# A graph attention layer with a dense 4096 x 4096 mask: half of each mask unit's transposes move from TensorE to the DMA queue in the last two chunks

## What is computed

```
h = relu(layernorm(x))
Wh = h @ W                                   # 4096 x 128
e  = leaky((Wh @ a1)[:, None] + (Wh @ a2)[None, :])   # leaky slope 0.2
e  = where(adj > 0, e, -9e15)                # adj: 4096 x 4096 int32, 64 MB
out = x + elu(softmax(e, axis=1) @ Wh)
```

## Time and profile before

| | |
|---|---|
| median of 3 runs | 248.27 us (248.07 to 249.45) |
| the profiled execution | 247.97 us |
| its span, first to last instruction | 246.2 us |
| PE, DVE, ACT, POOL busy | 92%, 80%, 69%, 24% |
| transfers of `adj` | 64 of 1 MB |

### The profile page before, as it was taken

The page is one execution under the profiler, slowest core; times in us unless marked ns, Lnnn a source line. Parts: engine busy times, 40 slices in busy tenths (PEclk is TensorE's granted clock), DMA queues, the critical chain, the costliest instruction groups (busy, mean ns, idle before and its releaser), DMA issues.

```text
span 246.2 us, 8267 instructions
## 1 busy us (share of the span) xinstructions
PE 227.2 (92%) x3736; PEld 221.2 (90%) x3736; DVE 196.3 (80%) x259; ACT 169.8 (69%) x149; POOL 59.0 (24%) x48
## 2 busy tenths in 40 slices
PE   6958999599999999999999999999999999999770
PEld 2748899599999999999999999999999999999770
DVE  4997988437776898889888988898889888988935
ACT  3699975696799999994996679219976795020051
POOL 3647027798000070300000560000003700040000
PEclk9997999999999999999999999999999999999996
DMA  6999999999999999999999999999999200020002
GB/s 216 352 387 387 385 388 386 386 319 337 304 333 325 335 388 386 386 385 385 397 387 386 388 386 388 386 386 376 385 387 384 89 3 0 3 88 3 0 3 91
DMA packets 36521, 71.92 MB, mean 292 GB/s; under 512 B 1282, under 2 KB 1924, under 8 KB 36484
## 3 DMA queue, kind: packets, MB, share of 16 engines
q1 hardware_dynamic: 35520, 69.74, 78.6%
q10 hardware_dynamic: 964, 1.64, 1.8%
HBM read 69.27 MB, written 2.10 MB: 290 GB/s over the span
## 4 chain that ended last, share of the span: by engine, by line
PE 77%; DVE 10%; issue 4%; POOL 4%; ACT 2%; DMA 1%; DVEq 0%; POOLq 0%
PE acc L834 21%; PE acc L835 21%; PE acc L836 21%; PE mask_t L817 11%; DVE words L610 3%; POOL v L330 2%; POOL val L333 2%; DVE stats L547 1%; DMA x_sb<-in_x_dram 1%; PE acc L805 1%; ACT v L508 1%; PE acc L796 1%; DVE wh_sb L573 1%; PE mask_t L785 1%; DVE hp L718 1%
## 5 line engine op out<-in xcount | busy, mean ns | idle before, releaser
L610 DVE SCALAR_TENSOR_TENSOR words<-g_row,gq_word,mask_t 128x1024 f32<-128x1024 f32 x128 | 161.1, 1277 | 36.7 <-PE acc L836 18.8
L834 PE MATMUL acc<-val,words 128*128 128x129 f16 x992 | 170.6, 220 | 1.2 <-DVE num L618 0.9
L835 PE MATMUL acc<-val,words 128*128 128x129 f16 x992 | 170.6, 220 | 0.0
L836 PE MATMUL acc<-val,words 128*128 128x129 f16 x992 | 170.6, 220 | 0.0
L420 ACT ACTIVATE mask<-raw,step_bias 128x2048 uint8<-128x2048 int32 x63 | 121.7, 1993 | 21.9 <-DVE x_sb L626 13.5
L834 PEld LDWEIGHTS acc<-val,words 128*128 128x128 f16 x992 | 97.1, 98 | 1.5 <-DVE words L610 1.0
L835 PEld LDWEIGHTS acc<-val,words 128*128 128x128 f16 x992 | 97.1, 98 | 0.1
L836 PEld LDWEIGHTS acc<-val,words 128*128 128x128 f16 x992 | 97.1, 98 | 0.0
L817 PE MATMUL mask_t<-ident_b,mask 128*128 128x128 bf16 x512 | 34.7, 222 | 1.4 <-ACT mask L420 1.4
L817 PEld LDWEIGHTS mask_t<-ident_b,mask 128*128 128x128 bf16 x512 | 30.8, 100 | 1.6 <-ACT mask L420 1.5
L358 POOL TENSOR_TENSOR hp<-num,rz 128x1024 f32<-128x1024 f32 x3 | 5.7, 1898 | 106.3 <-DVE rz L621 106.3
(11 more groups left out here) (94 smaller groups left out, 147.1 us busy)
## 6 DMA issues: line engine op xcount, KB each, us to landing
raw<-in_adj_dram SPq DMA_DIRECT2D x64, 1024.0 KB, 13.8
x_sb<-in_x_dram SPq DMA_DIRECT2D x8, 256.0 KB, 5.7
out_dram<-x_sb ACTq DMA_DIRECT2D x3, 512.0 KB, 7.5
out_dram<-x_sb SPq DMA_DIRECT2D x2, 128.0 KB, 1.9
out_dram<-x_sb SPq DMA_DIRECT2D x1, 192.0 KB, 2.0
w_sb<-in_L_gnn_W_dram ACTq DMA_DIRECT2D x1, 64.0 KB
out_dram<-x_sb SPq DMA_DIRECT2D x1, 64.0 KB, 1.7
a_sb<-in_L_gnn_a_dram ACTq DMA_DIRECT2D x1, 1.0 KB
```

The lines of the kernel that those rows point to most:

```text
L610: nc.vector.scalar_tensor_tensor(words[:, q], g_row[:, c * CHUNK:(c + 1) * CHUNK], gq_word[:, 1, t:t + 1], maskt_bytes[:, u % 2, q // 2, : ...
L834: nc.tensor.matmul(acc_tile(t), high, val[:, tile, 0, 0:V], start=first and t % PT == 0, stop=False, skip_group_check=True)
L835: nc.tensor.matmul(acc_tile(t), high, val[:, tile, 1, 0:V], start=False, stop=False, skip_group_check=True)
L836: last = nc.tensor.matmul(acc_tile(t), low, val[:, tile, 0, 0:V], start=False, stop=False, skip_group_check=True)
```

## The change

For units 16 to 31 (chunks 2 and 3; `BESIDE = 2 * U` = 16 is the first of them) PE transposes only the first of the two halves of the bytes. The other half, 128 partitions x 1024 two-byte pairs (256 KB), is transposed by a DMA from `mask` to `h_t`, which SP issues. Words 0 and 1 of a unit still come from PSUM, words 2 and 3 now from `h_t`, which is in SBUF and is a ring of 4 units. For this the pairs of the two halves are kept apart in `mask`, for all units: ACT (and DVE, for the very first half-unit) writes them through a strided view, and PE reads them without a stride.

New waits: SP issues the transpose of unit n between the two loads of unit n + 4, when ACT has finished unit n and DVE all words of unit n - 4; the last four stand behind all loads. DVE waits for it before word 2. ACT waits, before it writes the bytes of unit n, for the transpose of unit n - 4. PE's turn of unit n waits for word 1 of unit n - 2 instead of word 3.

```
+            def turn_beside(n):
+                sp.wait_ge(words_ready, BT * (n - RING + 1))
+                sp.dma_start(beside_pairs[:, n % RING], mask_pairs[:, n % RING, 1].rearrange("p t j -> p (t j)"), transpose=True
+                             ).then_inc(beside[n % RING], 16)
...
                         sp.wait_ge(act_bytes, 2 * (n - RING) + k)
+                    if n - RING >= BESIDE and k == 1:
+                        turn_beside(n - RING)
                     load_raw(n, k)
+            for n in range(C * U - RING, C * U):
+                sp.wait_ge(act_bytes, 2 * n + 1)
+                turn_beside(n)
...
+                if n >= BESIDE + RING:
+                    act.wait_ge(beside[u % RING], ((n - BESIDE) // RING) * 16)
-                nc.scalar.activation(mask[:, u % RING, k * BT:(k + 1) * BT], raw[:, u % RING, k * BT:(k + 1) * BT], ACT.Sigmoid,
+                nc.scalar.activation(mask_half(u % RING, k), raw_half(u % RING, k), ACT.Sigmoid,
...
+                if n >= BESIDE and q >= 2:
+                    if q == 2:
+                        dve.wait_ge(beside[n % RING], ((n - BESIDE) // RING + 1) * 16)
+                    turned_bytes = beside_bytes[:, n % RING, :, q % 2]
+                else:
+                    turned_bytes = maskt_bytes[:, u % 2, q // 2, :, q % 2]
...
-                for h in range(2):
+                for h in range(2 if n < BESIDE else 1):
                     for t in range(CT):
-                        last = nc.tensor.transpose(maskt_pairs[:, u % 2, h, t * P:(t + 1) * P], mask_pairs[:, u % RING, t, :, h], ident_b[:])
+                        last = nc.tensor.transpose(maskt_pairs[:, u % 2, h, t * P:(t + 1) * P], mask_pairs[:, u % RING, h, t], ident_b[:])
```

More of the change, by code:

```diff
@@ L48, in bass_graph_attention @@
     U = NB
+    BESIDE = 2 * U
     V = F + 1
@@ L74, in bass_graph_attention @@
         raw = sb("raw", [P, RING, CT, BLOCK], I32)
-        mask = sb("mask", [P, RING, CT, BLOCK], U8)
+        mask = sb("mask", [P, RING, 2, CT, BLOCK // 2], U8)
         words = sb("words", [P, WORDS, CHUNK], F32)
@@ L136, in bass_graph_attention, with raw_half, mask_half @@
         gq_word_h = gq_word[:].bitcast(F16).rearrange("p u (t e) -> p u t e", e=2)
-        mask_pairs = mask[:].bitcast(BF16).rearrange("p s t (j h) -> p s t j h", h=2)
+        mask_pairs = mask[:].bitcast(BF16)
         maskt_pairs = mask_t[:].bitcast(BF16)
         maskt_bytes = mask_t[:].bitcast(U8).rearrange("p s h (i e) -> p s h i e", e=2)
+        beside_pairs = h_t[:].bitcast(BF16).rearrange("p s (t i) -> p s t i", i=P)
+        beside_bytes = h_t[:].bitcast(U8).rearrange("p s (i e) -> p s i e", e=2)
+        def raw_half(s, k):
+            return raw[:, s, k * BT:(k + 1) * BT].rearrange("p t (j h e) -> p (t j) h e", h=2, e=2)
+        def mask_half(s, k):
+            return mask[:, s, :, k * BT:(k + 1) * BT].rearrange("p h t (j e) -> p (t j) h e", e=2)
         def acc_tile(t):
@@ L162, in bass_graph_attention @@
         turned = sem("turned")
+        beside = [sem(f"beside{s}") for s in range(RING)]
         words_ready = sem("words_ready")
@@ L609, in weights @@
                 t = u * BT + q
+                if n >= BESIDE and q >= 2:
[4 more added lines that the diff above has]
+                    turned_bytes = maskt_bytes[:, u % 2, q // 2, :, q % 2]
                 nc.vector.scalar_tensor_tensor(words[:, q], g_row[:, c * CHUNK:(c + 1) * CHUNK], gq_word[:, 1, t:t + 1],
-                                               maskt_bytes[:, u % 2, q // 2, :, q % 2], ALU.max, ALU.mult).then_inc(words_ready, 1)
+                                               turned_bytes, ALU.max, ALU.mult).then_inc(words_ready, 1)
             def take_sums(c):
@@ L639, in _ @@
             dve.wait_ge(raw_in[0][0], 16)
-            nc.vector.tensor_scalar(mask[:, 0, 0:BT], raw[:, 0, 0:BT], 0, None, ALU.is_gt).then_inc(first_bytes, 1)
+            nc.vector.tensor_scalar(mask_half(0, 0), raw_half(0, 0), 0, None, ALU.is_gt).then_inc(first_bytes, 1)
             make_words(0, 1, 3)
@@ L811, in turn @@
                 pe.wait_ge(act_bytes, 2 * n + 1)
-                if n >= 2:
+                if n >= BESIDE + 2:
+                    pe.wait_ge(words_ready, 4 * (n - 2) + 2)
+                elif n >= 2:
                     pe.wait_ge(words_ready, 4 * (n - 1))
-                for h in range(2):
+                for h in range(2 if n < BESIDE else 1):
                     for t in range(CT):
-                        last = nc.tensor.transpose(maskt_pairs[:, u % 2, h, t * P:(t + 1) * P], mask_pairs[:, u % RING, t, :, h], ident_b[:])
+                        last = nc.tensor.transpose(maskt_pairs[:, u % 2, h, t * P:(t + 1) * P], mask_pairs[:, u % RING, h, t], ident_b[:])
                 last.then_inc(turned, 1)
```

## The result

| | before | after |
|---|---|---|
| median | 248.17 us (247.93 to 249.45) | 365.66 us (365.34 to 371.56) |
| the profiled execution, its span | 247.97, 246.2 us | 365.58, 363.8 us |
| ratio, 95% interval | | 1.4725 (1.4677 to 1.4772) |

The kernel is 47% slower, where a gain of 2.4% was forecast, and the time lies far outside the range of 240.5 to 264. The 371.56 is one execution at a lower granted clock (0.64, the others 0.87 to 0.89) and isn't in the ratio. The page after, against the earlier trace rows: the shares, with the slices of ACT, of PE's granted clock and of the DMA engines.

A forecast was written before the change was run, and what follows sets the result against it. PE was taken as the bound, 6.33 us a unit. Saved transposes -7.1, chunk starts +0.2 and late DMA transposes +0.8 gave -6.1 us, so a median of 242.2 us from 248.27; range 240.5 to 264.

The forecast's parts named there:

- ACT and the first half-unit: ACT's and the first DVE byte writes through the strided view: unchanged at 1.94 us for ACT or slower, taken as 0.
- The bound beside it: ACT's byte-writing instruction: slower writes matter only above 2.6 us each; chance 0.02.
- 1.1 us kept for it: DVE's first half-unit instruction: a start up to 1.1 us later if the view halved its speed; taken as 0.
- The rival that gave 385 us: DMA queue: a transpose holds it like four loads, 10.8 us each, +137 us; chance 0.05.
- The price of a transpose: DMA queue: each transpose takes 1.0 us from the 16 engines, in time up to 0.93, so 0.8 us in all.
- The draining rival: DMA queue empties around each transpose: 2.8 us each, +15 us, 264 us; chance 0.19, shared with other costs.
- the prediction's own sum: Whole kernel: -7.1 us of PE transposes, +0.2 for chunk starts, +0.8 for late DMA transposes, -6.1 us in all.
- The critical unit: Unit 27: its transpose must land before word 2, which allows up to 0.93 us for each transpose.
- the rival of a slower DVE: DVE becomes the bound if SBUF words take 0.2 us more: 5.99 us a unit, 243.8 us; within a shared 0.12.
- The engines don't run dry: 0: SP's queue: a load issued 4 us later costs nothing, as 11 us of work is queued ahead.
- the 0.2 us kept for it: PE's first product of a chunk waits for the first sum: 0.1 us on each of two chunks.
- ACT's new wait: ACT waits for the transpose of unit n - 4 before writing: costs nothing, with 20 us to spare.

The follow-up runs named there:

- e1: The changed kernel with its new mask layout kept, but PE turning both halves in all 32 units and no DMA transposes: 365.98 us, ratio 1.4758.
- e3: The changed kernel with bytes written densely, half 0 then half 1, and all transposes on PE, none by DMA: 248.11 us, ratio 1.0014.
- e2: The changed kernel with only the write order changed, all pairs of half 0 before half 1; DMA transposes stay for units 16 to 31: 255.49 us, ratio 1.0289.
- the four kernels: The changed kernel with dense writes and DMA transposes from unit 16, 20, 22 or 24 on: 255.49, 253.25, 244.35 and 245.20 us.
- v2: The changed kernel with dense writes and DMA transposes only for units 20 to 31: 253.25 us, ratio 1.0190.
- v1: The changed kernel with dense writes and DMA transposes only for units 22 to 31: 244.35 us, ratio 0.9861.
- e6: e2 with each unit's DMA transpose sent a second time, into a scratch buffer that nothing reads: 289.93 us in the one execution.

## Why the prediction was wrong, point by point

**The step that failed** is in "ACT and the first half-unit": "No row shows a strided byte output; the input and the count are the same, so I take 0." It took +2.87 us for each of 63 instructions. The bound beside it was right: "it matters only above 2.6 us each", and 4.86 is above. In its place the runs show ACT as the bound: e1, with the layout alone, takes 365.98 us; e3, with the same layout written in dense runs, 248.11. What was wrong was the 0, with a chance of 0.02 for ACT above 2.6 us, and a range that didn't take it in. DVE's instruction was suspected, with 1.1 us kept for it (it took 1.56 more); ACT's, of the same view and 63 times as many, had no place in the range. The bound weighed ACT at the pace of chunks 2 and 3 only, and the layout changes all 32 units.

**The rival that gave 385 us** isn't borne out by the nearness of its number. It had a transpose take 10.8 us of the queue, and e1 has no transpose and takes 366. The price of 1309 ns for a block that the Trainium skill has in "VectorE: DVE Perf Modes", section "The three transpose paths", can't be multiplied by eight: eight blocks took 3.1 to 5.5 us from issue to landing in the changed kernel, and 2.3 us of the queue in e2, 0.91 of these for the data.

**The price of a transpose**, t = 1.0 us, is the second error, hidden by the first. The part that was worked out from packet sizes was right (0.91 us of data against 1.0). The pause of 1.25 us was not in it, and t is 2.3, with 2.3 to 3.1 over the four kernels. The draining rival came near with its 2.8, but its mechanism, "a transpose starts only when the loads ahead have landed", isn't what the packets show: the first half of a transpose follows the loads directly, and the pause is inside it. That "Advanced Engine Details and Errata" of the Trainium skill, section "X-Bar Transpose (TRN2)", has a transpose as fast as a regular DMA isn't borne out here: its data move at 283 to 289 GB/s against 384, and the queue loses 2.3 us where the estimate from that section was 0.7. With t = 2.3 the prediction's own sum gives -7.1 + 12 x (2.3 - 0.93) = +9.3 us; e2's profiled execution is 9.6 above that of before, its median 7.5 above. The t put in is read from that same trace, so this checks the sum and not the price; and PE loses the time at units 19 to 24, not at unit 27.

**The critical unit** was misread as well. The sum takes unit 27, by its word 2. But in unit 24, the first of a chunk, the sums stand behind word 2, and PE's first product waits for them. In the prediction's own terms its transpose lands at 191.6 - 3 x 5.45 + 9 t = 175.3 + 9 t and word 2 must start at 208.6 - 3 x 6.33 - 10 x 0.445 - 2 x 1.36 - 0.5 = 182.0, so the limit is t = 0.75 and not 0.93, and at t = 1.0 the price is 2.3 us and not 0.8. v2 stalls at this place. A smaller slip is in the rival of a slower DVE: 5.69 us of words and (1.55 + 1.22) / 8 of sums and result are 6.04 us for a unit, not 5.99. The first adds 1.5 us to the forecast, the second concerns a rival only. And PE's granted clock wasn't full in all but the first and last slices: the fourth reads 7, on which nothing rests.

**"The engines don't run dry: 0"** was wrong. The 11 us of work queued ahead were there, but the issue itself can hold SP for 5 to 11 us, which no row of before could show, and in v2 it used them up.

**What held.** PE was the bound before, and a unit falls from 6.33 to 5.89 us once ACT and the queue keep up (v1, e2). Words from SBUF take 1281 ns against 1278 in the changed kernel, up to 1320 in v1; DVE never was the bound. The arithmetic with t = 2.2 put v1 within 0.8 us of its time. PE's first product of a chunk waits for the sums as before (0.9 us in all, in v1 too), so the 0.2 us kept for it isn't seen. ACT's new wait costs nothing in the changed kernel, but in e2 ACT waits 13.6 us for transposes, where the prediction had given it 20 us to spare.

## What to carry to other kernels

A new layout is paid by whoever writes it, in every unit and not only in those that profit: price the producer's access pattern first, in runs of bytes between jumps, and if it must write runs of under 4 bytes to several places, let it walk one place after the other and read with a stride instead. A transpose by DMA isn't priced by its bytes: put it where the queue has slack, count a pause of all engines with it (1.25 us here), and add the time for which it holds the engine that issues it. Before a unit is called the critical one, look at the first unit of a chunk, where more work stands behind the same wait. A bound that the prediction works out and then takes at zero without a row should keep its chance and its end of the range, above all if it multiplies by the number of units.

## What the hardware showed that I had not expected

- ACT: 2048 numbers written as bytes in 2.00 us if they are dense (2.56 if every fourth byte is written), in 4.83 us if each pair jumps, 9.39 if each byte does; 4.6 to 4.7 ns for a jump with under 4 bytes, at most 1.9 ns with 4. DVE's one instruction shows it too (1217 against 2780 ns).
- All 16 DMA engines pause for 1.25 us between the two halves of a transpose of 256 KB that stands among loads, though loads are queued, even in another queue. Two in a row share one (e6), and two and a half passed without one at the end of v1.
- The issue of a transpose takes 1.25 us of SP where the queue is short, and mostly 4 to 11 us behind queued loads.
- PE's granted clock went to 0.50 behind an idle stretch of 4.5 us and stayed there for some 3 us (v2, 193 to 196 us). Shorter waits didn't always lower it: in e2 it was 1.00 from 152 to 177 us, where PE was idle for 3.0 us in all.
